# Second attention layer put into a software-pipelined order; GpSimd widens the reciprocals

## The chip, the cores and the metric

The kernel runs on one core of a Trainium2 chip. The metric is device time in microseconds (us). The core has five engines with a queue each: TensorE (PE), VectorE (DVE), ScalarE (ACT), GpSimd (POOL), and SyncE (SP), which issues the transfers. Each takes its instructions strictly in order and waits on semaphores for the others.

## The reference

16 entries of 128 rows by 512 go through two cross-attention layers. Layer 0 (16 heads, keys from the context and the entry itself) ends in a residual and a GELU MLP; its result is `y`. Layer 1, the one that the change touches, is a grouped attention with 32 query heads of 16 and 8 key heads:

```python
q = hidden_state @ Wq + bq
k = encoder_hidden_state @ Wk + bk
v = encoder_hidden_state @ Wv + bv
...
scores = jnp.einsum('bkgld,bksd->bkgls', q, k) * scale
scores = scores + encoder_attention_mask[:, :, None, :, :]
attn = jax.nn.softmax(scores, axis=-1)
out = jnp.einsum('bkgls,bksd->bkgld', attn, v)
...
out = out @ Wo + bo
x = out + hidden_state
mu = jnp.mean(x, axis=-1, keepdims=True)
var = jnp.var(x, axis=-1, keepdims=True)
return (x - mu) * jax.lax.rsqrt(var + EPS) * gamma + beta
```

## The kernel before

The program has three parts, one after the other with a barrier between: `attention` (layer 0), `mlp` and `second_attention` (layer 1). Products of fp32 are made of three passes over high and low halves (`split_product`, line 162). The weights of layer 1 are split into halves at its head (`take_hi` on ACT, `take_lo` on DVE).

`second_attention` works entry by entry. For entry e, in order of the data:

- `turn`: PE transposes the rows of `y` (line 1661), ACT writes `hThi` (1419), DVE `hTlo` (1505).
- `query`: PE makes 12 products (162), DVE adds the bias into `Qn` (1512). `turn_query`: PE transposes (1676), ACT and DVE write `QThi`, `QTlo`.
- `context`: PE makes 12 products for K and V, DVE writes `Cn` and `V` (1525, 1527). `turn_context`: PE transposes (1690), ACT writes `KThi` (1430), DVE `KTlo` (1534).
- `scores` in two rounds (1700), each filling four PSUM banks `S`. A round has four steps, so an entry has steps 0 to 7. In each step DVE adds the mask and takes the maximum (`mask_max`, 1548), ACT takes four exponentials with their sums (`exp`, 1441), PE transposes the probabilities (`probs`, 1710) into bank `O` or `T`, and DVE (1561, even steps) or ACT (1449, odd steps) copies them to `pT`.
- For each round: DVE takes the reciprocal of the sums (`invert`, 1555), PE transposes it (`inverse`, 1720), ACT copies it to `inv` (`spread`, 1455), PE multiplies with `V` (`values`, 1730), DVE scales (`attended`, 1568), POOL splits into `aThi` and `aTlo` (1376, 1378).
- `output`: 12 PE products in two halves (1743), DVE adds the residual (`res`, 1575), which POOL has prepared (`residual`, 1367). DVE takes the moments (1580 to 1591), POOL does three Newton steps (`root`, 1388), DVE normalises (`norm`, 1597), POOL applies gamma and beta (`affine`, 1395, 1397), SP stores.

Outside `S`, `O` and `T` two PSUM banks, `G` (the tiles J), are shared by all the rest. Each user waits for the semaphore of the former user's reader; in the kernel before, these waits are written out by hand.

What sets the order is a function `period(b)` on each engine, a hand-written list with operations of the entry before b, of b itself and of the one or two after it; `all_periods` runs it for b = -1 to 16, in a loop for the middle ones. The reciprocal is written 16 times wide by DVE itself, since the transposed copy is wanted on 16 rows for each head:

```python
nc.vector.reciprocal(rec[r][:, :, :], den[r][:, :].unsqueeze(2).broadcast_to([P, RC * EIGHT, DH1]))\
    .then_inc(rec_ready, 1)
```

Of the kernel before, what the change touches and what calls it, by code (L numbers as in the profile page):

```python
# [33 lines left out]
P = 128  # L34
# [10 lines left out]
SB = 4  # L45
# [1178 lines left out]

def all_periods(eng, period):

    for n in (-1, 0, 1):
        period(Entry(n))
    with eng.Fori(0, (B - 4) // 2) as it:
        period(Entry(2, it))  # L1230
        period(Entry(3, it))
    for n in (B - 2, B - 1, B):
        period(Entry(n))


def second_attention(nc, top, staging, ident, handed, banks, mask, q_b, k_b, v_b, o_b, norm_w, norm_b, out):
# [14 lines left out]
    with st:  # L1251
# [19 lines left out]
        rec = [sb(f"rec{r}", [P, RC * EIGHT, DH1]) for r in range(ROUNDS)]  # L1271
# [15 lines left out]
        a_seen, moments_seen, scores_seen = map(sem, ("a_seen", "moments_seen", "scores_seen"))  # L1287
# [6 lines left out]
        SMALL = 3  # L1294

# [8 lines left out]
        with nc.Block() as block:  # L1304

            @block.sync
            def _(sp):
                def load_context(e):
                    for h in range(2):
# [3 lines left out]
                def load_mask(e):  # L1313
                    sp.dma_start(madd[e.s][:, :], mask[e.index(), 0]).then_inc(mask_loaded[e.s], 16)

                def load_rows(e):
                    sp.dma_start(y_rows[e.s][:, :], kept_y[e.index()]).then_inc(y_loaded[e.s], 16)
# [4 lines left out]

                def period(b):
                    if b.exists() and b.plus(2).exists():
                        sp.wait_ge(resid_ready, b.count(1, 1))
                        sp.wait_ge(turned, b.count(1, 1))
                        load_rows(b.plus(2))
                        sp.wait_ge(c_full, b.count(1, 1))
                        load_context(b.plus(2))
                    if b.plus(-2).exists():  # L1330
                        store(b.plus(-2))
                    if b.exists() and b.plus(2).exists():
                        sp.wait_ge(masked, b.count(STEPS, STEPS))
                        load_mask(b.plus(2))
# [16 lines left out]
                store(Entry(B - 1))  # L1351
# [4 lines left out]
            def _(pool):  # L1356
# [22 lines left out]

                def root(e):  # L1380
# [18 lines left out]
                def period(b):  # L1399
                    if b.plus(-2).exists():  # L1400
                        root(b.plus(-2))
                    if b.plus(-1).exists():
                        attended(b.plus(-1), 1)
# [629 lines left out]
```

## Time and profile before

| | |
|---|---|
| median of 3 runs | 1276.95 us (1273.9 to 1278.49) |
| the profiled execution | 1279.8 us |
| its span | 1278.0 us |
| PE busy | 1121.2 us (88%) |
| DVE busy | 735.7 us (58%) |
| ACT busy | 658.9 us (52%) |
| POOL busy | 310.3 us (24%) |
| DMA, mean | 56 GB/s |

The shares are means over three different stages; the layer in question is the last third of the span. Busy time of PE counts matmuls that overlap by their starts, with modelled ends. Idle time in a wait is put down to the instruction that released it.

### The profile page before, as it was taken

How to read it: one execution, taken by the hardware profiler on the slowest of the kernel's cores; microseconds unless marked ns; L12 is line 12 of the kernel's file. 1: busy time of each engine (PE TensorE's matmuls, PEld its weight loads, DVE VectorE, ACT ScalarE, POOL GpSimd, SP SyncE). 2: the span in 40 equal slices, each digit the busy share in tenths (PEclk: the TensorE clock that was granted, in tenths of full speed). 3: DMA queues.
4: the chain of work that ended last, by engine and by line, in shares of the span. 5: the costliest groups of instructions: out<-in, count | busy, mean ns of one | idle time of the engine just before them, and what ended most of it. 6: DMA issues, size and time to landing. Idle time of an engine off the chain costs nothing. (4 is left out here: it accounts for less than half of the span.)

```text
span 1278.0 us, 27329 instructions
## 1 busy us (share of the span) xinstructions
PE 1121.2 (88%) x8976; PEld 935.1 (73%) x8976; DVE 735.7 (58%) x2667; ACT 658.9 (52%) x2220; POOL 310.3 (24%) x475
## 2 busy tenths in 40 slices
PE   4899999999999975999999999996778778778774
PEld 3788888888888854898989989985556556556553
DVE  4577777777776755422212212215678778788784
ACT  4455555555555544533333333325677677677672
POOL 1223333332332331000000000000133333333334
PEclk8999999999999987999999999997889989989987
DMA  6212111112111005211001101404111111111100
GB/s 242 86 55 69 45 43 43 43 47 81 44 43 43 26 17 174 90 50 50 30 20 49 50 0 49 116 17 116 32 59 36 53 52 35 56 49 35 45 10 25
DMA packets 65349, 71.10 MB, mean 56 GB/s; under 512 B 7056, under 2 KB 41104, under 8 KB 65296
## 3 DMA queue, kind: packets, MB, share of 16 engines
q1 hardware_dynamic: 65296, 70.42, 17.5%
q8 instruction: 30, 0.49, 0.2%
q14 instruction: 23, 0.19, 0.1%
HBM read 49.43 MB, written 20.97 MB: 55 GB/s over the span
## 5 line engine op out<-in xcount | busy, mean ns | idle before, releaser
L689 POOL TENSOR_TENSOR pr<-pr,rec 128x512 f32<-128x512 f32 x128 | 130.6, 1042 | 297.2 <-DVE rec L947 297.2
L1441 ACT ACTIVATE pr<-pr,nmax 128x128 f32<-128x128 f32 x512 | 198.1, 392 | 0.8
L1921 ACT ACTIVATE g_m<-J,b_part_m 128x256 f32<-128x256 f32 x128 | 60.6, 474 | 217.9 <-PE J L162 217.9
L791 ACT ACTIVATE pr<-pr,nmax 128x256 f32<-128x256 f32 x256 | 126.6, 501 | 4.1 <-DVE nmax L936 4.0
L1548 DVE CUSTOM_DVE_ANT_0 pr<-S,madd 128x128 f32<-128x128 f32 x512 | 115.7, 284 | 14.3 <-PE S L1700 10.3
L1898 POOL TENSOR_TENSOR resid_m<-resid_m,b_all_m 128x512 f32<-128x512 f32 x16 | 23.1, 1464 | 329.7 <-DMA resid_m<-in_x 329.7
L1441 ACT ACTIVATION_READ_ACCUMULATOR pr<-pr,nmax 128x1 f32 x512 | 98.4, 192 | 0.0
L936 DVE CUSTOM_DVE_ANT_0 pr<-S,madd 128x256 f32<-128x256 f32 x256 | 92.6, 418 | 8.2 <-PE S L1127 8.1
L162 PE MATMUL J<-wqhi,hThi 128*128 128x512 f32 x128 | 65.1, 508 | 22.6 <-DVE wqlo L150 11.3
L162 PE MATMUL J<-nT0hi_m,uphi_m 128*128 128x256 f32 x256 | 73.2, 286 | 9.8 <-DVE uplo_m L150 8.9
L162 PE MATMUL J<-hThi,wkhi 128*128 128x256 f32 x256 | 75.4, 294 | 5.9 <-DVE wvlo L150 5.9
L162 PE MATMUL J<-nT0hi_m,uplo_m 128*128 128x256 f32 x256 | 72.7, 284 | 0.0
L162 PE MATMUL J<-nT0lo_m,uphi_m 128*128 128x256 f32 x256 | 72.6, 283 | 0.0
L1710 PE MATMUL T<-ident,pr 128*128 128x128 f32 x256 | 42.0, 289 | 34.5 <-ACT pr L1441 34.5
L162 PE MATMUL J<-hThi,wklo 128*128 128x256 f32 x256 | 72.0, 281 | 0.0
L162 PE MATMUL J<-hTlo,wkhi 128*128 128x256 f32 x256 | 72.0, 281 | 0.0
L162 PE MATMUL J<-nT1hi_m,uphi_m 128*128 128x256 f32 x256 | 71.8, 280 | 0.0
L162 PE MATMUL J<-nT1hi_m,uplo_m 128*128 128x256 f32 x256 | 71.6, 280 | 0.0
L162 PE MATMUL J<-nT1lo_m,uphi_m 128*128 128x256 f32 x256 | 71.5, 279 | 0.0
L1145 PE MATMUL S<-ident,pr 128*128 128x128 f32 x512 | 62.9, 277 | 0.0
L162 PE MATMUL J<-wqlo,hThi 128*128 128x512 f32 x128 | 61.8, 483 | 0.0
L1455 ACT ACTIVATE inv<-J 128x256 f32<-128x256 f32 x32 | 12.3, 384 | 94.2 <-PE J L1720 94.2
(232 smaller groups left out, 3323.1 us busy)
## 6 DMA issues: line engine op xcount, KB each, us to landing
staged<-in_L_xattn_mlp_w SPq DMA_DIRECT2D x16, 512.0 KB, 5.1
rows<-in_ctx SPq DMA_DIRECT2D x16, 256.0 KB, 2.8
rows<-in_x SPq DMA_DIRECT2D x16, 256.0 KB, 3.0
kept_c<-hThi SPq DMA_DIRECT2D x16, 256.0 KB, 2.6
kept_c<-hTlo SPq DMA_DIRECT2D x16, 256.0 KB, 2.8
kept_n<-n_out SPq DMA_DIRECT2D x16, 256.0 KB, 2.4
n_in<-kept_n SPq DMA_DIRECT2D x16, 256.0 KB, 3.7
resid_m<-in_x SPq DMA_DIRECT2D x16, 256.0 KB, 2.9
```

What stands on the lines that cost most here:

```text
L162: mm = nc.tensor.matmul(out, stationary(a, k), moving(b, k), start=first and k == 0 and (a, b) == PASSES[0], stop=last and k == chunks - 1 ...
L689: pool.tensor_tensor(part, part, by.unsqueeze(2).broadcast_to([P, per_bank, keys]), ALU.mult).then_inc(normed, 1)
L791: last = nc.scalar.activation(part, part, ACT.Exp, bias=nmax[slot][:, at], scale=-1.0, accum_out=den[slot][:, at])
L936: last = nc.vector.tensor_tensor_reduce(pr[slot][:, j, cols], S[j][:, cols], madd[s][:, :], -1.0, FAR, ALU.add, ALU.min, nmax[slot][:, j * ...
L1145: mm = nc.tensor.transpose(S[j][:, to * P:(to + 1) * P], pr[slot][:, j, q * P:(q + 1) * P], ident[:, :])
L1441: last = nc.scalar.activation(pr[k][:, i, :], pr[k][:, i, :], ACT.Exp, bias=nmax[k][:, i:i + 1], scale=-1.0, accum_out=den[r][:, at:at + 1])
L1455: nc.scalar.activation(inv[r][:, :], G[r][:, 0:RC * R], ACT.Copy).then_inc(r_spread, 1)
L1548: last = nc.vector.tensor_tensor_reduce(pr[k][:, i, :], S[j][:, i * R:(i + 1) * R], madd[e.s][:, :], -1.0, FAR, ALU.add, ALU.min, nmax[k][ ...
L1710: mm = nc.tensor.transpose(PT[t][:, i * R:(i + 1) * R], pr[k][:, i, :], ident[:, :])
L1898: pool.tensor_tensor(resid[t][:, :], resid[t][:, :], b2_all[:, :], ALU.add)\
L1921: nc.scalar.activation(g[slot][:, :], J[j][:, 0:PR], ACT.Gelu_apprx_tanh, bias=b1_part[:, f, :]).then_inc(J_taken[j], 1)
```

## The change

1. Each operation of the layer gets a place in the period and an entry, from two ahead (`turn`, `query`, `turn_query`, `context`) over one ahead (`turn_context`, the first steps) to one behind (`output`, `moments`, `root`) and two behind (`norm`, `affine`, `store`). `all_periods` now runs from -2 to 17, and nothing is left outside it.
2. A table (`HOME`) gives each operation one of the two banks: `values` of round 0 moves from the bank of `inverse` 0 to the other, `turn_context` too, `context` and `output` change to bank 0. PE's waits for a free bank are derived from the table and the order (`free`). `values` 0 no longer waits for `inv`.
3. `invert` gives 16 values per partition, and POOL copies them 16 wide (`widen`), for PE's `inverse`.
4. The bank of a copy of step k is written as `k % 2`; which engine copies is as before.
5. SP's loads of mask, rows and context are placed by entry, with waits of their own.

```diff
+def at(b, ahead, operation, *which):
+
+    e = b.plus(ahead)
+    if e.exists():
+        operation(e, *which)
...
-    for n in (-1, 0, 1):
+    for n in range(-2, 4):
         period(Entry(n))
...
-        rec = [sb(f"rec{r}", [P, RC * EIGHT, DH1]) for r in range(ROUNDS)]
+        rec = [sb(f"rec{r}", [P, RC * EIGHT]) for r in range(ROUNDS)]
+        wide = [sb(f"wide{r}", [P, RC * EIGHT, DH1]) for r in range(ROUNDS)]
...
+        HOME = dict(turn=1, query=0, turn_query=0, context=0, turn_context=1, inverse0=0, inverse1=1, values0=1,
+                    values1=1, output=0)
+        ORDER = (("turn", 2), ("output", -1), ("turn_context", 1), ("inverse0", 0), ("values0", 0), ("query", 2),
+                 ("inverse1", 0), ("turn_query", 2), ("values1", 0), ("context", 2))
...
                 def period(b):
...
+                    if not first_two(b.plus(1)):
+                        at(b, 1, load_mask)
+                    if not first_two(b.plus(2)):
+                        at(b, 2, load_rows)
+                    if not first_two(b.plus(2)):
+                        at(b, 2, load_context)
+                    at(b, -2, store)
...
+                def widen(e, r):
+                    pool.wait_ge(rec_ready, e.count(ROUNDS, r + 1))
+                    wait(pool, r_full, e.count(ROUNDS, r - 1))
+                    pool.nop().then_inc(rec_seen, 1)
+                    pool.tensor_copy(wide[r][:, :, :], rec[r][:, :].unsqueeze(2).broadcast_to([P, RC * EIGHT, DH1]))\
+                        .then_inc(rec_wide, 1)
...
+                    at(b, -1, attended, 1)
+                    at(b, 1, residual)
+                    at(b, 0, widen, 1)
+                    at(b, -2, affine)
+                    at(b, 0, attended, 0)
+                    at(b, -1, root)
+                    at(b, 1, widen, 0)
...
-                    nc.vector.reciprocal(rec[r][:, :, :], den[r][:, :].unsqueeze(2).broadcast_to([P, RC * EIGHT, DH1]))\
-                        .then_inc(rec_ready, 1)
+                    wait(dve, rec_wide, e.count(ROUNDS, r - 1))
+                    nc.vector.reciprocal(rec[r][:, :], den[r][:, :]).then_inc(rec_ready, 1)
...
-                turn(Entry(0))
                 for u in QUERY + (CONTEXT,):
                     staging.take_lo(nc, dve, u, targets[u])
                 dve.wait_ge(consts_loaded, 96)
                 dve.wait_ge(prepared, 3)
                 all_periods(dve, period)
-                norm(Entry(B - 1))
...
                 def values(e, r):
-                    pe.wait_ge(r_spread, e.count(ROUNDS, r + 1))
+                    free(f"values{r}", e)
...
+                    at(b, 2, turn)
+                    at(b, 0, probs, 3)
+                    at(b, -1, output, 0)
+                    at(b, 1, turn_context)
+                    at(b, 0, probs, 4)
+                    at(b, -1, output, 1)
+                    at(b, 0, probs, 5)
+                    at(b, 1, scores, 0)
+                    at(b, 0, probs, 6)
+                    at(b, 0, inverse, 0)
+                    at(b, 0, values, 0)
+                    at(b, 0, probs, 7)
+                    at(b, 2, query)
+                    at(b, 1, probs, 0)
+                    at(b, 0, inverse, 1)
+                    at(b, 1, scores, 1)
+                    at(b, 2, turn_query)
+                    at(b, 1, probs, 1)
+                    at(b, 0, values, 1)
+                    at(b, 1, probs, 2)
+                    at(b, 2, context)
```

Three places show what stands in the queues. On ACT, in the last period before the loop, around `inv` of round 0; before:

```order
L1441 ACTIVATE pr_1,den_1<-pr_1,nmax_1 128x128 x3
L1449 ACTIVATE pT_1<-T 128x512 [waits o_full_1,p_full1_1]
L1441 ACTIVATE pr_1,den_1<-pr_1,nmax_1 128x128 [waits masked_1]
L1441 ACTIVATE pr_1,den_1<-pr_1,nmax_1 128x128 x3
L1430 ACTIVATE KT0hi<-J,parity 128x128 [waits ct_full_1]
L1430 ACTIVATE KT0hi<-J,parity 128x128
L1455 ACTIVATE inv_1<-J 128x256 [waits a_scaled_1,r_full_1]
L1441 ACTIVATE pr_1,den_1<-pr_1,nmax_1 128x128 [waits masked_1]
L1441 ACTIVATE pr_1,den_1<-pr_1,nmax_1 128x128 x3
L1449 ACTIVATE pT_1<-T 128x512 [waits o_full_1,p_full1_1]
```

and now (L1466 is the exponential, L1474 the copy of probabilities, L1480 `inv`):

```order
L1466 ACTIVATE pr_1,den_1<-pr_1,nmax_1 128x128 [waits masked_1]
L1466 ACTIVATE pr_1,den_1<-pr_1,nmax_1 128x128 x3
L1474 ACTIVATE pT_1<-T 128x512 [waits o_full_1,p_full1_1]
L1466 ACTIVATE pr_1,den_1<-pr_1,nmax_1 128x128 [waits masked_1]
L1466 ACTIVATE pr_1,den_1<-pr_1,nmax_1 128x128 x3
L1480 ACTIVATE inv_1<-J 128x256 [waits a_scaled_1,r_full_1]
L1466 ACTIVATE pr_1,den_1<-pr_1,nmax_1 128x128 [waits rec_ready_1,masked_1]
L1466 ACTIVATE pr_1,den_1<-pr_1,nmax_1 128x128 x3
L1466 ACTIVATE pr_1,den_1<-pr_1,nmax_1 128x128 [waits masked_1]
L1466 ACTIVATE pr_1,den_1<-pr_1,nmax_1 128x128 x3
L1474 ACTIVATE pT_1<-T 128x512 [waits o_full_1,p_full1_1]
L1466 ACTIVATE pr_1,den_1<-pr_1,nmax_1 128x128 [waits masked_1]
```

Before, `inv` stood ahead of the exponentials of step 6, and `KThi` ahead of `inv`; now the exponentials of step 7 are ahead of it, and behind it come those of the next entry, steps 0 and 1.

On PE, the same place of the program, behind the scores of the next entry's first round; before (T is a bank for odd steps, O for even ones):

```order
L1700 MATMUL S<-KT0lo,QT0hi 128x256 x4
L1700 MATMUL S<-KT0hi,QT0lo 128x256 x4
L1720 MATMUL J<-ident,rec_1 128x128 [waits rec_ready_1,a_scaled_1]
L1720 MATMUL J<-ident,rec_1 128x128
L1710 MATMUL T<-ident,pr_1 128x128 [waits copied1_1,exped_1]
L1710 MATMUL T<-ident,pr_1 128x128 x3
L1730 MATMUL J<-pT_1,V_1 32x256 [waits copied1_1,copied0_1,r_spread_1]
L1730 MATMUL J<-pT_1,V_1 32x256 x7
L1710 MATMUL O<-ident,pr_1 128x128 [waits copied0_1,exped_1]
L1710 MATMUL O<-ident,pr_1 128x128 x3
L1661 MATMUL J<-ident,y_rows 128x128 [waits res_ready_1,y_loaded1]
```

and now:

```order
L1707 MATMUL S<-KT0lo,QT0hi 128x256 x4
L1707 MATMUL S<-KT0hi,QT0lo 128x256 x4
L1717 MATMUL O<-ident,pr_1 128x128 [waits copied0_1,exped_1]
L1717 MATMUL O<-ident,pr_1 128x128 x3
L1724 MATMUL J<-ident,wide_1 128x128 [waits rec_wide_1,res_ready_1]
L1724 MATMUL J<-ident,wide_1 128x128
L1734 MATMUL J<-pT_1,V_1 32x256 [waits copied1_1,copied0_1,k_ready_1]
L1734 MATMUL J<-pT_1,V_1 32x256 x7
L1717 MATMUL T<-ident,pr_1 128x128 [waits copied1_1,exped_1]
L1717 MATMUL T<-ident,pr_1 128x128 x3
L162 MATMUL J<-wqhi,hThi 128x512 [waits r_spread_1,h_ready_1]
```

`values` had to wait for `r_spread`, ACT's copy of the transposed reciprocals; now for `k_ready`, the former reader of its bank. `turn` is gone from the end of the period, and the query products of the entry two ahead stand behind the transposes of step 7.

On DVE, at the head of the layer; before:

```order
L1501 TENSOR_REDUCE parity<-ident 128x1 x2
L1505 TENSOR_TENSOR hTlo<-J,hThi 128x512 [waits h_hi_1]
L150 TENSOR_TENSOR wqlo<-staged,wqhi 128x1024 [waits staged_hi] x2
L150 TENSOR_TENSOR wclo<-staged,wchi 128x1024 [waits staged_hi]
L1512 TENSOR_TENSOR Qn<-J,bq_all 128x8x4x16 [waits q_full_1,prepared_1,consts_loaded_1]
L1517 SCALAR_TENSOR_TENSOR QT0lo<-J,QT0hi 128x512 [waits q_hi_1]
```

and now:

```order
L1513 TENSOR_REDUCE parity<-ident 128x1 x2
L150 TENSOR_TENSOR wqlo<-staged,wqhi 128x1024 [waits staged_hi] x2
L150 TENSOR_TENSOR wclo<-staged,wchi 128x1024 [waits staged_hi]
L1517 TENSOR_TENSOR hTlo<-J,hThi 128x512 [waits h_hi_1,prepared_1,consts_loaded_1]
L1524 TENSOR_TENSOR Qn<-J,bq_all 128x8x4x16 [waits q_full_1]
L1529 SCALAR_TENSOR_TENSOR QT0lo<-J,QT0hi 128x512 [waits q_hi_1]
```

`hTlo` of entry 0 stood first; now it is behind the three splits of weights, and the wait for all constants has moved from `Qn` to it.

## Rows read from the trace of the kernel before

**Rows 1.** Stages. Columns: window, us, busy us (x instructions) per engine, TensorE clock, DMA share, GB/s
```profile
860.10:898.22 38.12, 21.55 (x135) 16.90 (x136) 23.36 (x93) 19.84 (x64) 3.10 (x5) 0.76 0.38 111
898.22:1233.17 334.95, 265.25 (x2254) 199.71 (x2254) 260.42 (x1225) 233.49 (x1036) 111.68 (x251) 0.92 0.14 44
1233.17:1278.00 44.83, 26.21 (x188) 16.60 (x188) 23.81 (x100) 19.98 (x90) 20.43 (x51) 0.71 0.05 19
```

**Rows 2.** Waits in 898.22 to 1233.17: engine, line, waited for: total us, times, longest
```profile
ACT inv L1455 <- PE J L1720: 88.4, 28, 3.9
...
DVE hTlo L1505 <- ACT hThi L1419: 43.9, 14, 4.4
...
PE T L1710 <- ACT pr L1441: 31.5, 14, 2.3
```

**Rows 3.** Groups by line, second layer: busy us, mean ns | idle before
```profile
L1441 ACT ACTIVATE pr<-pr,nmax 128x128 f32<-128x128 f32 x512 | 198.1, 392 | 0.8
...
L1555 DVE RECIPROCAL rec<-den 128x256 f32<-128x256 f32 x32 | 55.9, 1746 | 0.0
...
L1376 POOL CAST aT1hi<-an 128x256 fp32r<-128x256 f32 x16 | 6.5, 407 | 77.3 <-DVE an L1568 72.9 <-issue 4.3
...
L1585 DVE TENSOR_SCALAR stat<-stat 128x1 f32<-128x1 f32 x16 | 2.5, 154 | 0.6
```

**Rows 4.** Timeline of ACT, one period: start, us, instruction, idle before and releaser
```profile
1115.23 0.38 ACT L1455 ACTIVATE inv<-J 128x256 f32<-128x256 f32 x1 [3.49 <-PE J L1720]
```

**Rows 5.** Timeline of PE, same period
```profile
1108.95 0.47 PE L1743 MATMUL J<-wohi,aT0hi 128*128 128x512 f32 x1 [0.37 <-issue]
...
1111.89 0.39 PE L1743 MATMUL J<-wolo,aT0hi 128*128 128x512 f32 x1
1112.12 0.40 PE L1743 MATMUL J<-wohi,aT0lo 128*128 128x512 f32 x1
1113.84 0.39 PE L1700 MATMUL S<-KT0hi,QT0hi 32*128 32x256 f32 x4 [1.33 <-DVE KT0lo L1534]
...
1115.66 1.07 PE L1730 MATMUL J<-pT,V 128*32 128x256 f32 x16
...
1120.66 0.65 PE L1710 MATMUL T<-ident,pr 128*128 128x128 f32 x4 [2.30 <-ACT pr L1441]
```

**Rows 6.** That period in seven windows, columns as in the stages
```profile
1098.69:1102.10 3.41, 3.41 (x9) 2.65 (x9) 3.41 (x15) 1.65 (x8) 2.61 (x12) 0.50 0.00 0
...
1115.75:1119.17 3.42, 2.07 (x24) 1.19 (x24) 0.37 (x5) 2.65 (x11) 0.00 (x0) 1.00 0.55 186
1119.17:1122.58 3.41, 1.51 (x8) 1.14 (x9) 3.15 (x17) 3.41 (x18) 0.67 (x2) 1.00 0.13 44
sum 23.89, PE 18.91 PEld 14.22 DVE 18.79 ACT 16.73 POOL 8.48; mean PE 2.70 PEld 2.03 DVE 2.68 ACT 2.39 POOL 1.21
```

**Rows 7.** Tile y_rows in 898 to 1233: landing of its loads
```profile
DMA to landing us min/median/max: 2.6/2.7/2.7
```

**Rows 8.** Timeline of DVE, head of the second layer
```profile
863.06 0.69 DVE L1505 TENSOR_TENSOR hTlo<-J,hThi 128x512 fp32r<-128x512 f32 x1 [0.95 <-ACT hThi L1419]
...
872.43 0.69 DVE L1512 TENSOR_TENSOR Qn<-J,bq_all 128x512 f32<-128x512 f32 x1 [4.93 <-DMA nb_all<-in_L_xattn_beta]
```

**Rows 9.** Timeline of PE, same stretch
```profile
866.42 0.79 PE L162 MATMUL J<-wqhi,hThi 128*128 128x512 f32 x1 [4.03 <-DVE wqlo L150]
...
870.69 0.40 PE L162 MATMUL J<-wqhi,hTlo 128*128 128x512 f32 x1
...
879.02 0.39 PE L1700 MATMUL S<-KT0hi,QT0hi 32*128 32x256 f32 x4 [1.36 <-DVE KT0lo L1534]
```

**Rows 10.** Timeline of POOL, last entries
```profile
1262.85 1.29 POOL L1395 TENSOR_TENSOR fin<-nrm,nw_all 128x512 f32<-128x512 f32 x1
...
1269.03 0.46 POOL L1388 TENSOR_TENSOR stat<-stat 128x1 f32<-128x1 f32 x2 [3.54 <-DVE stat L1591]
...
1272.01 0.20 POOL L1388 TENSOR_TENSOR stat<-stat 128x1 f32<-128x1 f32 x1
```

More of the change, by code:

```diff
@@ L1294, in second_attention, with bank @@
         SMALL = 3
+        HOME = dict(turn=1, query=0, turn_query=0, context=0, turn_context=1, inverse0=0, inverse1=1, values0=1,
+                    values1=1, output=0)
+        ORDER = (("turn", 2), ("output", -1), ("turn_context", 1), ("inverse0", 0), ("values0", 0), ("query", 2),
+                 ("inverse1", 0), ("turn_query", 2), ("values1", 0), ("context", 2))
+        EMPTIED = dict(turn=(h_ready, 1, 1), query=(q_added, 1, 1), turn_query=(q_ready, 1, 1), context=(c_ready, 1, 1),
+                       turn_context=(k_ready, 1, 1), inverse0=(r_spread, 2, 1), inverse1=(r_spread, 2, 2),
+                       values0=(a_scaled, 2, 1), values1=(a_scaled, 2, 2), output=(res_ready, 1, 1))
+        def bank(use):
+            return G[HOME[use]]
         u0, end = staging.first[2], staging.first[3]
@@ L1652, in _, with free @@
                 all_periods(dve, period)
-                norm(Entry(B - 1))
             @block.tensor
             def _(pe):
+                def free(use, e):
+                    at_ = [name for name, _ in ORDER].index(use)
+                    b = e.plus(-ORDER[at_][1])
+                    for back in range(1, 3 * len(ORDER)):
+                        periods, n = divmod(at_ - back, len(ORDER))
+                        name, ahead = ORDER[n]
+                        user = b.plus(periods + ahead)
+                        if HOME[name] == HOME[use] and user.exists():
+                            sem_, per, more = EMPTIED[name]
+                            pe.wait_ge(sem_, user.count(per, more))
+                            return
                 def turn(e):
                     pe.wait_ge(y_loaded[e.s], e.uses(16))
-                    wait(pe, res_ready, e.count(1, -2))
+                    free("turn", e)
                     for k in range(KC):
-                        mm = nc.tensor.transpose(G[1][:, k * R:(k + 1) * R], y_rows[e.s][:, k * P:(k + 1) * P],
+                        mm = nc.tensor.transpose(bank("turn")[:, k * R:(k + 1) * R], y_rows[e.s][:, k * P:(k + 1) * P],
                                                  ident[:, :])
@@ L1688, in turn_context @@
                     pe.wait_ge(c_ready, e.count(1, 1))
-                    pe.wait_ge(q_ready, e.count(1, 1))
-                    nc.tensor.transpose(G[0][:, 0:R], Cn[:, :], ident[:, :]).then_inc(ct_full, 1)
+                    free("turn_context", e)
+                    nc.tensor.transpose(bank("turn_context")[:, 0:R], Cn[:, :], ident[:, :]).then_inc(ct_full, 1)
                 def scores(e, r):
@@ L1775, in period @@
-                    if b.exists():
-                        probs(b, 4)
-                    if before.exists():
-                        output(before, 1)
-                    if after.exists():
-                        scores(after, 0)
-                    if b.exists():
-                        inverse(b, 0)
-                        probs(b, 5)
-                        values(b, 0)
-                        probs(b, 6)
-                    if b.plus(2).exists():
-                        turn(b.plus(2))
```

245 lines of the change are left out of this document (85 added, 160 removed).

## The prediction

> **What bounds the kernel now.** I read the stages first. The second layer's steady part, from the scores of entry 1 to those of entry 15, takes 334.95 us for 14 periods, 23.9 each, and the 860 us before the layer are two stages that the change leaves alone [rows 1]. In that part no engine is full: divided by 14, PE is busy 18.9 us a period, DVE 18.6, ACT 16.7, POOL 8.0. So the layer is not held by one engine's work but by the order in which three nearly equal engines wait for one another, and the waits say where [rows 2]: ACT stands 88.4 us in 28 waits of `inv` (6.3 a period) for PE's transpose of the reciprocals, DVE 43.9 us (3.1 a period) in `hTlo` for ACT, PE 31.5 us (2.2 a period) in the transposes of the last probabilities for ACT's exponentials. These are one circle. The reciprocal takes DVE 1.75 us [rows 3]; until it is done PE can't transpose it and ACT, which has `inv` next in its queue, does nothing [rows 4]; all exponentials behind it are late, so PE idles before step 7's transposes [rows 5], and `turn` is late for DVE.
>
> One thing comes on top: after the stretch in which PE does little but transposes and waits (1.51 us busy of 3.41), its clock drops from 2.4 to 1.2 GHz for 3.41 us, and the next period's query products run there [rows 6]. The other six windows of that period are at 1.00. PE was full in the slow one, so 1.7 of its 3.41 us are the price.
>
> **The change, part by part.**
> 1. *Reciprocal of 16 values, not 256.* Removes 2 x 1.746 us of DVE a period [rows 3]. The trace has no reciprocal of 16; its ends are a tiny DVE operation (0.154 us) and the old one (1.746). A sixteenth of the elements is nearest to the tiny one; I take 0.2. DVE's work: 18.6 - 3.5 + 0.4 = 15.5 us.
> 2. *GpSimd widens.* Two copies to 128x256 a period. Nearest row is the cast of 128x256, 0.41 us [rows 3]; POOL becomes 8.0 + 0.8 = 8.8 us, a third of its time. What stands behind them: `widen` 1 waits for the reciprocal with `affine` and `attended` 0 behind it, `widen` 0 stands behind the Newton steps (some 3.2 us). Both have several us before PE wants them, since the PE order puts `inverse` half a period later.
> 3. *The reciprocals' transpose no longer stands before ACT's next exponentials.* `inv` of round 1 moves behind steps 0 to 2 of the next entry, `inv` of round 0 behind step 7. The 6.3 us of ACT's waits go. ACT's work is unchanged: 16.7 us a period.
> 4. *`turn` and `query` two ahead, in one period; `values` of round 0 in the other bank.* PE's matmuls are the same. Its busy time of 18.9 us minus the 1.7 of the slow window is 17.2 us at full clock; matmul records overlap a little, so 17.2 is an upper end and 16.7 about a lower one.
> 5. *SP's loads.* Each is now issued behind `store` of an entry that waits for `affine`. By POOL's order `affine` ends some 12 us into a period and the rows are wanted by `turn` at the start of the next; landing takes 2.7 us at most [rows 7]. Hidden, with about 1 us to spare.
>
> The floor of the period is then 16.7 (ACT) to 17.2 (PE). I walked one new period, with these durations (an exponential step is 4 x 0.392 = 1.57 us [rows 3]; on PE four transposes 0.5, `values` 1.0, products of 512 columns 0.23 each from start to start [rows 5]), and met five places where PE can wait: `turn_context` for `hTlo` behind step 4's exponentials, `output` for `context` at the seam, `scores` of the next entry for `KTlo` (before: 1.33 us), transposes 7 for `exp` 7 (before: 2.30 us [rows 5]), `context` for `QTlo`. Each has another operation as cover and leaves 0 to 0.4 us. Counted from PE's `turn`, in us: output half 0 at 1.1, `turn_context` 2.6, transposes 4 at 2.7, output half 1 at 3.2, transposes 5 at 4.7, `scores` of the next entry at 5.4, transposes 6 at 6.3, `inverse` 0 and `values` 0 at 6.8 and 7.1, transposes 7 at 8.1, `query` from 8.6 to 11.4, then transposes 0, `inverse` 1 and `scores` 1 until 13.1, `turn_query`, transposes 1, `values` 1 and transposes 2 until 15.5, `context` until 17.0. ACT is through at 16.3 and DVE, which ends with `context`, at 17.6, that is 0.6 into the next. The walk closes at 17.0; it knows no sequencer time for the waits, of which PE showed 0.37 us before one output [rows 5]. With 0.5 us for such, I take **17.5 us a period**. The gain is 14 x (23.9 - 17.5) = 90 us.
>
> *Head.* All `turn` are now inside the periods, and DVE enters them after a wait for all six constants. So the first `hTlo`, at 863.1 before, runs when the constants are there, which was 872.4 [rows 8]. The query products (866.4 to 871.1 [rows 9]) start at about 873.1 and end at 877.8; before, their reader could start at 872.4. That is 5.4 us lost. `context` 0 then waits for the query's bank use (`q_ready`), 1.7 more, and entry 1's `turn` stands ahead of `turn_context` 0, 0.7 more. I take +7.5 us; the ends are +5.4, and +10 if entry 1's products, which were beside nothing else, hold the next scores up too.
>
> *Tail.* From scores of entry 15 to the end 44.8 us [rows 1]. `widen`, `affine` 13 and Newton 14 (2.6 and 3.2 us [rows 10]) now stand ahead of POOL's last split; against that, ACT's two waits of `inv` (6.3 us) fall away. I take -1.5, ends -6 and +5.
>
> Sum: 1278.0 - 90 + 7.5 - 1.5 = 1194.0 us span; with the 1.8 us around the span 1195.8 for this execution (1279.8). The median shown, 1276.95, is 0.22% below it: **1193 us**.
>
> **A rule that speaks against it.** What the rows show: the clock fell after a stretch with transposes, waits and four products [rows 6], and stayed up after one with 16 `values` products and eight transposes. The new period has as many transposes, but in the PE order never more than two such groups stand between products. So the sum has full clock. The Trainium skill (TensorE: Matmul & The Clock Gate, on transposes) says that transposes don't count as PE work for the clock. By that rule, the trace agreeing so far, a denser queue of transposes and idle moments need not keep the clock up; the next rival is what it would make.
>
> **The rivals.**
> - *A slow window in each period stays.* It costs 1.7 us of a PE that is now nearly full, so the period is 17.5 + 1.7 = 19.2 at most, 18.7 if the other waits hide in it; I take 18.9. For: the new stretch from step 5 to step 7 has only `scores` and `values` as products. Against: the window with `values` as its only products was followed by one at 1.00 [rows 6]. Time: 1193 + 14 x 1.4 = 1213.
> - *The interlocks are tighter than my walk.* Three engines at 88% or more of a period of 17.5, each strictly in order: any late one is everybody's. If the waits add 3 to 4 us to the floor in place of 0.5, the period is 20 to 21 and the time 1228 to 1242. For: the waits shown are all on another engine [rows 2], and three such engines were kept 5 us apart from their work before. Against: the places above have cover.
> - *Slower than before: GpSimd as the bound.* The widened copy reads each value 16 times, a form that the trace doesn't have. PE's `inverse` 1, the whole queue behind it and SP's loads behind `affine` hang on it. It decides once POOL's sum passes 23.8 us: (23.8 - 8.0) / 2 = 7.9 us a copy, 19 times the cast. At 8.2 us the period is 24.4, the time 1277 + 14 x 0.5 + 6 = 1290. Against: its longest operation in the layer takes 1.29 us, for two inputs of twice the size [rows 10].
> - *No difference.* It needs a period of 23.5 us, so that removed waits return elsewhere (the 1.7 us of the clock and 4 us of interlocks). Nothing in the rows points there.
>
> **How the numbers follow.** Forecast (period 16.9 to 18.1) 0.55, slow window 0.25, tight interlocks 0.15, no difference 0.02, slower 0.03. A measurement can tell 0.3%, 4 us. The low end is the floor period, 14 x 0.7 = 10 us below: 1183. The high end takes in the slow window with the dearer head: 1220. Faster 0.95, same 0.02, slower 0.03.
>
> **What would show it.** Right: in the profile after, scores of successive entries 17 to 18 us apart; a RECIPROCAL group near 0.2 us; ACT's wait for `inv` under 1 us a period; PE clock 1.0 in the steady part; first scores at about 887; POOL copies near 0.4 us. Wrong: a regular 0.50 window, PE waits for `hTlo`, `KTlo` or `y_rows` over 1 us a period, or POOL over 12 us a period.

## The result, and the profile after

The changed kernel takes **1179.33 us** (median of 4 runs, 1176.5 to 1182.09) against 1277.65 for the kernel before beside it: ratio 0.9236, 95% interval 0.9205 to 0.9266. The forecast was 1193, with a range from 1183 to 1220. The direction was right, and the time came out below the low end.

Stages of the profiled execution after (1182.09 us, span 1179.4), cut at the same events as [rows 1]: the entry-1 scores, the entry-15 scores, the end. Columns as there.

```profile
857.85:905.11 47.26, 24.25 (x142) 19.44 (x142) 23.13 (x94) 21.11 (x70) 3.49 (x6) 0.68 0.31 89
905.11:1139.48 234.37, 232.97 (x2252) 182.68 (x2252) 216.02 (x1224) 229.51 (x1038) 118.62 (x277) 0.99 0.19 62
1139.48:1179.40 39.92, 20.62 (x185) 13.38 (x184) 20.30 (x101) 18.59 (x86) 23.86 (x56) 0.86 0.07 27
```

The middle row is the result: 14 periods in 234.37 us, 16.74 each, where there were 334.95 us, 23.93 each. (The first of them takes 18.09 us; TensorE's granted clock in it is 0.52 until 909. The other 13 take 16.64 each.) PE is busy 232.97 of 234.37 us (99.4%), ACT 97.9%, DVE 92.2%. PE's sum came down from 265.25 to 232.97 us with the same instructions. About half of that is the clock: old_clock below has 267.02 us at full clock, of which its 84 extra products are about 19 (an estimate, 0.23 us each), so some 248 are left. The rest fits how records are counted, though no run isolates it: a product with a break behind it counts 0.39 us, one that is followed at once 0.23.

From PE's first `turn` of the layer (861.76 before, 859.51 after) the head to entry 1's scores took 36.5 us before and takes 45.6, +9.1. The tail went from 44.8 to 39.9, -4.9. Together: 1278.0 - 100.6 + 9.1 - 4.9 = 1181.6; the remaining 2.3 us lie ahead of the layer, in code that is the same in both.

What [rows 2] showed is gone. The waits of PE, and the longest ones of ACT and DVE, in the steady part after (engine, line, waited for: total us, times, longest); first PE:

```profile
PE J L1666 <- DMA y_rows<-kept_y: 0.6, 2, 0.4
PE J L1746 <- DVE V L1539: 0.2, 1, 0.2
```

then ACT:

```profile
ACT QT0hi L1449 <- PE J L1682: 2.4, 5, 1.1
ACT QT1hi L1449 <- PE J L1682: 1.0, 5, 0.2
ACT hThi L1444 <- PE J L1666: 0.5, 2, 0.3
ACT inv L1480 <- PE J L1724: 0.3, 1, 0.3
```

then DVE:

```profile
DVE Qn L1524 <- PE J L162: 7.5, 14, 1.2
DVE pr L1560 <- issue: 2.3, 6, 1.3
```

ACT's 88.4 us for `inv` are 0.3, DVE's 43.9 for `hTlo` 0.2, PE's 31.5 for the last exponentials none. The groups that answer to the reciprocal and the cast of [rows 3], steady part:

```profile
L1407 POOL COPY wide<-rec 128x256 f32<-128x256 f32 x28 | 11.1, 397 | 41.3 <-DVE rec L1568 39.0 <-POOL stat L1418 2.3
...
L1568 DVE RECIPROCAL rec<-den 128x16 f32<-128x16 f32 x28 | 6.9, 245 | 0.0
```

And one period in windows, as [rows 6]; the clock is 1.00 in all five, and PE is busy throughout in four of them:

```profile
1006.54:1009.95 3.41, 3.41 (x52) 2.51 (x52) 3.18 (x18) 3.41 (x17) 1.28 (x1) 1.00 0.00 0
1009.95:1013.36 3.41, 3.41 (x22) 2.65 (x21) 2.98 (x23) 3.41 (x18) 2.71 (x3) 1.00 0.00 0
1013.36:1016.77 3.41, 3.41 (x54) 2.53 (x54) 3.13 (x14) 3.28 (x16) 2.50 (x10) 1.00 0.47 130
1016.77:1020.18 3.41, 3.41 (x27) 3.21 (x26) 3.34 (x19) 3.41 (x14) 2.58 (x9) 1.00 0.54 196
1020.18:1023.59 3.41, 3.35 (x33) 2.55 (x34) 3.41 (x22) 3.41 (x19) 0.00 (x0) 1.00 0.00 0
```

### The profile page after: what moved, and what is told of

It is laid out like the page before. It is cut to its first block and busy times, and to the rows that moved or that the text cites. A ratio compares the mean times of both kernels' runs of the same rounds, so it can differ in the third digit from the quotient of the medians.

```text
span 1179.4 us, 27363 instructions
## 1 busy us (share of the span) xinstructions
PE 1086.9 (92%) x8976; PEld 918.5 (78%) x8976; DVE 688.2 (58%) x2667; ACT 654.9 (56%) x2220; POOL 321.0 (27%) x507
## 3 DMA queue, kind: packets, MB, share of 16 engines
q1 hardware_dynamic: 65296, 70.42, 18.9%
## 5 line engine op out<-in xcount | busy, mean ns | idle before, releaser
L1466 ACT ACTIVATE pr<-pr,nmax 128x128 f32<-128x128 f32 x512 | 199.1, 402 | 3.2 <-DVE nmax L1560 3.2
L1466 ACT ACTIVATION_READ_ACCUMULATOR pr<-pr,nmax 128x1 f32 x512 | 103.3, 202 | 0.0
L162 PE MATMUL J<-wqhi,hThi 128*128 128x512 f32 x128 | 56.0, 438 | 18.3 <-DVE hTlo L1517 10.9
L1145 PEld LDWEIGHTS S<-ident,pr 128*128 128x128 f32 x512 | 59.0, 144 | 2.2 <-issue 0.2
L162 PEld LDWEIGHTS J<-nT0hi_m,uphi_m 128*128 128x128 f32 x256 | 49.0, 192 | 12.9 <-issue 9.3
L162 PEld LDWEIGHTS J<-hThi,wkhi 128*128 128x128 f32 x256 | 48.6, 190 | 7.7 <-DVE wvlo L150 5.0
```

The lines of the kernel that those rows point to most:

```text
L162: mm = nc.tensor.matmul(out, stationary(a, k), moving(b, k), start=first and k == 0 and (a, b) == PASSES[0], stop=last and k == chunks - 1 ...
L1145: mm = nc.tensor.transpose(S[j][:, to * P:(to + 1) * P], pr[slot][:, j, q * P:(q + 1) * P], ident[:, :])
L1466: last = nc.scalar.activation(pr[k][:, i, :], pr[k][:, i, :], ACT.Exp, bias=nmax[k][:, i:i + 1], scale=-1.0, accum_out=den[r][:, at:at + 1])
```

## The experiments

**How they are read.** The second layer began anywhere from 856 to 867 us in these executions, in code that no edit touches. So the period is read from the trace of each (start of entry 1's scores to start of entry 15's, over 14), and the medians stand beside it where there were rounds; a time without a ratio is a single execution. How far a period repeats can be seen in new_head and new_head_tail, whose steady part is that of the changed kernel: 16.75 and 16.77 beside 16.74. Two theories stood against each other. *Order*: the old time went through waits in a circle, and the new period is PE's own work, with nothing on top. *Part*: the narrow reciprocal, or the clock, brought most of it.

### The parts of the change, alone

**old_narrow**: the order of before with the narrow reciprocal.

```diff
+                def widen(e, r):
...
+                    pool.tensor_copy(wide[r][:, :, :], rec[r][:, :].unsqueeze(2).broadcast_to([P, RC * EIGHT, DH1]))\
...
-                    nc.vector.reciprocal(rec[r][:, :, :], den[r][:, :].unsqueeze(2).broadcast_to([P, RC * EIGHT, DH1]))\
-                        .then_inc(rec_ready, 1)
+                    nc.vector.reciprocal(rec[r][:, :], den[r][:, :]).then_inc(rec_ready, 1)
```

GpSimd does `widen` of round 1 first in its period, and of round 0 ahead of `attended(b, 0)`.

> The order of before, with one part of the change alone: DVE takes the reciprocal of 16 values and GpSimd widens it. Theory (the time went through the circle of waits, PE's transpose of the reciprocals standing before ACT's next exponentials): the circle gets shorter by what leaves DVE in it, 1.75 - 0.25 - 0.40 = 1.1 us at each of two rounds, less what the two more hand-overs cost. The period falls from 23.9 us by 1 to 2.5 us, so 14 x 1 to 2.5 = 14 to 35 us less than before, about 1255; ACT still waits 4 to 5 us a period for its copy inv. Rival (the narrow reciprocal is what brought the gain, the order little): most of the 98 us, a time under 1215.

Measured: 1267.6 us, ratio 0.991 (0.9877 to 0.9943); period 23.20, 0.73 us less. The theory's lower end was missed, and the rival's gain of most of 98 us is far off. Why so little? ACT's wait in old_narrow, 899.59 to 1224.37:

```profile
ACT inv L1468 <- PE J L1733: 79.2, 28, 3.6
```

It hardly fell from 88.4. PE's timeline of the kernel before shows what the releaser's name hid:

```profile
1121.72 0.50 PE L162 MATMUL J<-wqhi,hThi 128*128 128x512 f32 x1 [0.41 <-DVE an L1568]
...
1125.88 0.45 PE L162 MATMUL J<-wqhi,hTlo 128*128 128x512 f32 x1
1126.17 0.60 PE L1710 MATMUL O<-ident,pr 128*128 128x128 f32 x4
1126.61 0.38 PE L1720 MATMUL J<-ident,rec 128*128 128x128 f32 x2
```

and DVE's, the reciprocal beside them:

```profile
1123.95 1.74 DVE L1555 RECIPROCAL rec<-den 128x256 f32<-128x256 f32 x1
```

The reciprocal ended at 1125.7, under twelve query products that stood ahead of its transpose in PE's queue until 1126.2. In this round (round 1) the 1.75 us of the reciprocal were nearly free: the wait was PE's order.

In round 0 too the transpose waited for something else. The reciprocal on DVE and the transpose on PE, in the kernel before:

```profile
1110.06 1.75 DVE L1555 RECIPROCAL rec<-den 128x256 f32<-128x256 f32 x1
...
1113.10 0.61 DVE L1534 SCALAR_TENSOR_TENSOR KT0lo<-J,parity,KT0hi 128x128 fp32r<-128x128 f32 x2
...
1114.75 0.44 PE L1720 MATMUL J<-ident,rec 128*128 128x128 f32 x2
```

It was done at 1111.8, and PE transposed it 2.9 us later, behind the scores that waited for `KT0lo` [rows 5]. `KT0lo` stands behind the reciprocal in DVE's queue, so the wide reciprocal did cost something here, but through DVE's own queue. In old_narrow DVE gets only a part of the 1.5 us back, because the copy behind the reciprocal then waits 0.85 us for PE; what is left is about the 0.73 us of the period:

```profile
1106.37 0.69 DVE L1574 COPY pT<-O 128x512 f32<-128x512 f32 x1 [0.85 <-PE O L1723]
```

**new_wide**: the new order with the wide reciprocal back on DVE (the reverse of the diff above).

> The new order with that one part undone: DVE writes the reciprocals wide again (1.75 us each), GpSimd widens nothing. Theory (the new period is at the floor of the busiest engine): DVE's 15.4 us a period become 15.4 + 2 x 1.5 = 18.4 us, more than PE's 16.6, so DVE sets the period at 18.4 to 18.9 us: 14 to 15 periods x 1.8 = 25 to 32 us slower than the changed kernel, about 1207. Rival (the order gives all of it and has room for the wide reciprocals): within 5 us of 1179. Second rival (the order closes only with the narrow reciprocal): a period over 20 us, over 1225.

Measured: 1213.72 us, ratio 0.9491 (0.9437 to 0.9545), period 18.73.

```profile
905.21:1167.43 262.22, 237.81 (x2251) 182.79 (x2250) 253.89 (x1224) 233.34 (x1038) 108.37 (x249) 1.00 0.17 55
```

The columns are as in the stages: PE, PEld, DVE, ACT, POOL. DVE, the third, is now 253.89 of 262.22 us, 97%, and sets the pace. The period is inside the expected 18.4 to 18.9; the time is 34 us above the changed kernel's, not 25 to 32, and 4.4 of them lie in the tail (44.27 against 39.92 us). Of the 7.19 us that the change takes from a period, the order alone gives 5.20 and the reciprocal alone 0.73; the other 1.26 are there only with both. The reciprocal is worth 1.99 us in the new order, because there DVE would be the fullest engine.

**old_clock**: the kernel before, with filler on PE before step 7's transposes; its result is overwritten.

```diff
+                def filler(e):
+                    pe.wait_ge(copied[1], e.count(SB, 3))
+                    for _ in range(6):
+                        nc.tensor.matmul(PT[1][:, :], wq[0][:, 0, 0:P], wq[0][:, 0, :], start=True, stop=True)
```

> The kernel before, with six products of 512 columns more a period (their result is never used, and is overwritten), which PE does while it would wait for the last exponentials. Theory A (the half-speed window of every period cost about 1.7 us beside the waits, and came after a stretch in which PE did little but transposes): the granted clock stays at 1.00 in the second layer and the period falls from 23.9 to about 22.2 us, 24 us less. Rival B (the window fell into the time that the circle of waits had to spare, or more work does not keep the clock up): the period stays at 23.9 us or grows by up to 1.4 us (the six products), 0 to +20 us.

Measured: 1268.18 us, ratio 0.9922 (0.9894 to 0.995), period 23.35, granted clock 0.99 in the steady part (0.92 before). More work on PE made the kernel faster. So the clock theory holds in kind, but the window cost 0.57 us a period here, not 1.7. The filler itself is not in that number: it fits into PE's wait before step 7's transposes, of which 12.2 us in 14 are left. What takes the place of the slow products is the wide reciprocal, for which PE's transpose now waits 5.8 us in 13 periods:

```profile
1097.05 0.44 PE L1725 MATMUL J<-ident,rec 128*128 128x128 f32 x2 [0.38 <-DVE rec L1555]
```

**old_narrow_clock**: both.

> The order of before with both edits at once, the narrow reciprocal widened by GpSimd and the six unused products a period on PE. Alone they gave 0.73 and 0.57 us a period. Theory (each hid the other: at ACT's wait for round 0 the wide reciprocal ended at 1125.7 and PE's query products, at half speed, at 1126.2, so that removing one leaves the other): together they give clearly more than the sum of 1.3, 2.0 to 3.0 us a period, 28 to 42 us, about 1243. Rival (they are independent): 1.3 us a period, about 1259. Second rival (the order itself is the limit, both are small change): under 1 us a period, over 1263.

Measured: 1247.2 us, ratio 0.976 (0.9712 to 0.9808), period 21.91: 2.02 us less, where 0.73 + 0.57 = 1.30 was the sum. The two hid each other, at the theory's lower end. The trace is of the fastest of the six executions (1238.5 us), so the medians matter here: against the kernel before they give 30.4 us for both, 10.8 and 10.2 for each alone, the same picture.

**old_spread_later**: the kernel before, ACT's `inv` one place later.

```diff
                         copy(before, 7)
                     if b.exists():
                         exp(b, 1)
+                        exp(b, 2)
                     if before.exists():
                         spread(before, 1)
                     if b.exists():
-                        exp(b, 2)
                         copy(b, 1)
                         exp(b, 3)
                     if after.exists():
...
                         for u in OUT:
                             staging.take_hi(nc, act, u, targets[u])
                     if b.exists():
-                        spread(b, 0)
                         exp(b, 6)
+                        spread(b, 0)
                         copy(b, 5)
                     if b.plus(2).exists():
                         turn(b.plus(2))
```

> The kernel before with ACT's copy inv one place later in both rounds: behind the next entry's third exponential step in place of before its third (round 1), and behind the copy of step 5 (round 0). Nothing else moves. Theory (the reciprocals' place in ACT's queue alone makes the circle): ACT has work while it would wait, its wait of 6.3 us a period falls by 1 to 3, and the period by 0.5 to 2 us, 7 to 28 us less. Rival (the wait is only moved: values of the same bank and DVE's attended wait for inv instead, and PE's transposes are as late as before): within 5 us of before.

(That text puts round 0's copy behind the copy of step 5; it is ahead of it, behind the exponentials of step 6, as the diff shows.)

Measured: 1267.27 us, ratio 0.9925 (0.9897 to 0.9953), period 23.01, 0.91 less. ACT's wait in 899 to 1230 halved,

```profile
ACT inv L1455 <- PE J L1720: 44.4, 27, 2.5
```

but of the 44 us that it lost only 13 came off the time. Removing part of a wait's total didn't bring that much off the time.

**old_three**: all three in the old order.

> The order of before with the narrow reciprocal, the six unused products a period, and ACT's copy inv one place later in both rounds. The first two together gave 2.0 us a period, the last alone 0.9. Theory (waits that hide one another: each edit gives more once the others are made): 3.3 to 4.5 us a period, a period of 19.5 to 20.6, about 1222. Rival (they add up): 2.9 us, a period of 21.0, about 1236. Second rival (they overlap, the remainder is held by another circle of the old order): under 2.5 us, a period over 21.4.

Measured: 1231.52 us, ratio 0.9638 (0.9602 to 0.9675), period 21.12: 2.81 us less, against 2.02 + 0.91 if they add up. So the theory of the text above (3.3 to 4.5) fails and its first rival holds: this pair adds up. (The medians, 48.8 us against 30.4 + 10.3, don't contradict it within their intervals.) The other 4.4 us down to 16.74 belong to the rest of the order: in old_three, 899 to 1180, these waits stand:

```profile
DVE hTlo L1518 <- ACT hThi L1432: 35.5, 14, 3.8
...
ACT hThi L1432 <- PE J L1674: 22.1, 14, 2.2
ACT inv L1468 <- PE J L1738: 21.2, 13, 1.7
DVE pT L1574 <- PE O L1723: 17.2, 26, 1.5
```

The first two are `turn`. Both orders do it for the entry two ahead, but on PE the old one has it behind step 6's transposes and the new one before those of step 3, three steps earlier. Whether its move alone takes these waits away was not tried.

### What bounds the new period

**new_pe_more**: four unused products more before step 0's transposes, `nc.tensor.matmul(PT[t][:, :], wq[0][:, 0, 0:P], wq[0][:, 0, :], start=True, stop=True)` each.

> The changed kernel with four products of 512 columns more a period on PE (their result is never used), 4 x 0.23 = 0.93 us by the rows. Theory (PE bounds the period, with no slack): the period grows by 0.93 to about 17.6 us, the time by about 14 us, and PE stays at 98 to 99% busy. Rival (the period closes through waits between the engines, and PE has cover): the period grows by under 0.4 us.

Measured: 1193.4 us, period 17.61, +0.87. PE busy 245.40 of 246.57 us. The theory holds.

**new_pe_less**: four products fewer.

```diff
-                    split_product(nc, bank("query")[:, :], lambda h, k: hT[h][:, k, :], lambda h, k: wq[h][:, k, :], KC)
+                    for k in range(KC):
+                        for h in range(2):
+                            mm = nc.tensor.matmul(bank("query")[:, :], hT[0][:, k, :], wq[h][:, k, :],
+                                                  start=k == 0 and h == 0, stop=k == KC - 1 and h == 1)
```

> The changed kernel with one of three passes of the query product left out (the pass of the low half of the hidden rows; the output is a little less exact): 4 products, 0.93 us of PE a period. Theory (PE bounds now, ACT at 16.4 us a period is right behind it): the period falls only to ACT's sum, 16.4 to 16.6 us, the time by 2 to 5 us, and PE shows waits for ACT. Rival (ACT has more room than its busy time says): the period falls by the full 0.93 us to 15.8, 13 us less.

Measured: 1182.42 us, period 16.38, -0.36 (its layer began at 866.95, 7.4 us later than in the changed kernel, which hides the gain in its time).

```profile
910.05:1139.37 229.32, 221.00 (x2195) 172.07 (x2195) 216.62 (x1224) 228.18 (x1038) 118.47 (x277) 0.99 0.19 63
```

ACT, the fourth column, 228.18 of 229.32 us, takes over. Between PE's bound and ACT's lie 0.36 us.

**new_act_more**: two copies of a bank more on ACT, `nc.scalar.activation(spare[k // 2][:, :], PT[k % 2][:, :], ACT.Copy)` in steps 1 and 3.

> The changed kernel with two copies of a transpose bank to an unused tile more a period on ACT, about 0.5 us each. Theory (ACT has 0.3 us a period to spare under PE's 16.7): the period becomes ACT's new sum, 16.4 + 1.0 = 17.4 us, so about +0.7 us a period, +10 us, and PE waits for exponentials. Rival (PE alone sets the period, and ACT's waits have more cover): within 4 us of 1179.

Measured: 1191.66 us, period 17.41, +0.67; ACT busy 242.24 of 243.76 us. ACT can be filled to 99.4% as PE can.

**new_dve_more**: two copies more on DVE, ahead of the real copies of steps 0 and 2.

```diff
+                    if k in (0, 2):
+                        nc.vector.tensor_copy(spare[k // 2][:, :], PT[k % 2][:, :])
                     nc.vector.tensor_copy(pT[r][:, j, :, :, :].rearrange("p c a k -> p (c a k)"), PT[k % 2][:, :])
```

> The changed kernel with two copies of a transpose bank to an unused tile more a period on DVE, about 0.6 us each. Theory (DVE has 1.3 us a period to spare): its sum becomes 15.4 + 1.2 = 16.6 us, just PE's; the time grows by 0 to 6 us. Rival (each late DVE operation is everybody's): the whole 1.2 us a period, +17 us.

Measured: 1196.08 us, period 17.58, +0.84. A miss: DVE's busy time left 1.3 us a period, its sum rose by only 1.0 (230.07 against 216.02 us), and the period by 0.84. Two runs ask why.

**new_dve_free**: two additions behind the real copies, from data in SBUF, so that no bank is held.

```diff
                         .then_inc(copied[k % 2], 1)
+                    if k in (0, 2):
+                        nc.vector.tensor_tensor(spare[k // 2][:, :], wq[0][:, 0, :].bitcast(F32), wq[0][:, 1, :].bitcast(F32), ALU.add)
```

> The changed kernel with two additions of 128x512 to an unused tile more a period on DVE, at the same places as the two copies that cost 0.84 us a period, but behind the real copy of the bank and from other data, so that no bank is held longer. Theory A (the copies cost by holding PE's transpose banks for 0.6 us more): now under 0.3 us a period, about 1183. Rival B (DVE's queue has only 0.5 us of waiting in it, the rest of its idle time is gaps between dependent small operations that no work can fill): again 0.6 to 0.9 us a period, 9 to 13 us in all.

Measured: 1195.45 us, period 17.56, +0.82. The held bank is out.

**new_dve_seam**: one such addition, in `query` before `dve.wait_ge(q_full, e.count(1, 1))`.

> The changed kernel with one such addition a period, just before DVE's query, where it waits 0.54 us for PE. By either theory that wait takes it up: the period grows by 0 to 0.2 us, under 3 us in all. Against (DVE has no room at any place): 0.6 us, 9 us in all.

Measured: 1180.27 us, period 16.85, +0.11. DVE's wait for the query (7.5 us in the changed kernel) is 0.6 here:

```profile
DVE Qn L1526 <- PE J L162: 0.6, 1, 0.6
```

So DVE has room at one place, the 0.54 us in front of `Qn`, and next to none elsewhere. In new_dve_free that wait is still there:

```profile
DVE Qn L1525 <- PE J L162: 7.3, 14, 1.0
```

Work put behind that wait doesn't use it. What it does instead shows on PE, in new_dve_more:

```profile
PE J L1749 <- DVE V L1540: 5.1, 13, 0.8
```

(5.0 us in new_dve_free, 0.2 in the changed kernel.) `V` is the end of DVE's period, and PE's `output` needs its bank. So the added work makes `V` late, PE and its next query late with it, and the wait in front of `Qn` is as long as before. This reading fits the three runs; no run moves `V` alone.

**new_samebank**: `values0=0` in the table of banks for `values0=1`.

> The changed kernel with its other table entry put back: the values of round 0 go to the bank of the inverse of round 0, as before, and not to the other one. Theory (PE is full and each of its waits is paid in full): values 0 follows inverse 0 in the same bank and must wait until ACT has copied the inverse, some 0.7 to 1.2 us, and a transpose stands behind it; the period grows from 16.7 by 0.7 to 1.5 us, 10 to 22 us slower than the changed kernel, 1190 to 1200. Rival (there are 0.3 us of slack on ACT and 1.3 on DVE, PE catches up elsewhere): within 4 us of 1179.

Measured: 1200.04 us, ratio 0.9386 (0.9337 to 0.9435), period 18.09, +1.35. PE's timeline of one period:

```profile
1052.14 1.07 PE L1734 MATMUL J<-pT,V 128*32 128x256 f32 x16 [0.89 <-ACT inv L1480]
...
1054.01 0.47 PE L162 MATMUL J<-wqhi,hThi 128*128 128x512 f32 x1 [0.21 <-DVE an L1581]
```

PE waits 0.89 + 0.21 us at the two places foreseen; the whole costs 20.7 us. Putting back that one number in the table costs a fifth of the change's gain.

### Head and tail, and a kernel that beats both

**new_head**: only the three constants loaded first are awaited by DVE, at its first `query`.

```diff
+        early = sem("early")
...
+                    first = frm is q_b or frm is k_b or frm is v_b
-                    sp.dma_start(to, frm.partition_broadcast(P)).then_inc(consts_loaded, 16)
+                    sp.dma_start(to, frm.partition_broadcast(P)).then_inc(early if first else consts_loaded, 16)
...
+                    if e.it is None and e.n == 0:
+                        dve.wait_ge(early, 48)
```

> The changed kernel, with its head mended: DVE waits before its first operations of the layer for no constants, and at its first query for the three constants that are loaded first, not for all six. Theory (the head's loss is DVE's wait of 6.2 us for the last constant): the first hTlo comes about 6 us earlier and with it the first scores, 6 us less: ratio to the changed kernel 0.995, about 1173.5. Rival (PE or ACT is late next in the head: takes of the weights, context behind the query): under 3 us.

Measured: 1173.74 us over 6 runs, ratio 0.9176 (0.9138 to 0.9214). From the layer's first `turn` to entry 1's scores: 39.5 us, 6.1 less than in the changed kernel, as expected. DVE's timeline in the changed kernel showed the wait:

```profile
870.24 0.69 DVE L1517 TENSOR_TENSOR hTlo<-J,hThi 128x512 fp32r<-128x512 f32 x1 [6.17 <-DMA nb_all<-in_L_xattn_beta]
```

Three of the head's 9.1 us remain. They go with the new place of `query` and `turn` there; no run takes them apart.

**new_head_tail**: the same head, and this order in the last two periods.

```diff
+                        at(b, -1, attended, 1)
+                        at(b, 0, widen, 1)
+                        at(b, 0, attended, 0)
+                        at(b, -2, affine)
+                        at(b, 0, attended, 1)
+                        at(b, -1, root)
```

> The same head, and at the end another order on GpSimd: in the last two periods the splits of entry 15's rows go before the affine of entry 13 and the Newton steps of entry 14. Theory (PE's last two output halves each wait 1.8 us for the split, behind 2.6 and 3.2 us of such work): both waits go, and the end comes 3 to 5 us earlier than in the one before: about 1169.5. Rival (affine and Newton of the entries before are now late, and hold DVE's norm and the last output): 0 to +3 us.

Measured: 1172.41 us over 6 runs, ratio 0.9171 (0.9133 to 0.921). Its tail takes 38.65 us, 1.3 less than new_head's 39.93, not 3 to 5; the medians (1.3 us apart, intervals almost the same) can't tell the two kernels apart, so this gain is the trace's alone. PE's waits for the splits (1.76 and 1.81 us) became one of 1.42, but in DVE's timeline the norm of entry 14, which stands ahead of the last output, now waits longer for GpSimd's Newton steps (4.32 in the changed kernel):

```profile
1162.17 0.55 DVE L1624 TENSOR_SCALAR nrm<-res,stat 128x512 f32<-128x512 f32 x1 [5.69 <-POOLq L1422]
```

Theory and rival were both half right. By the medians this kernel is 7 us faster than the changed one and 105 us faster than before. Against the changed kernel the two intervals of the ratio still touch (0.9205 and 0.921), so the 7 us rest on the traces as well: 6.0 us in the head (39.57 against 45.60) and 1.3 in the tail.

## Why the prediction was right or wrong

**What bounds the kernel.** Right: an order of waits, and no engine's work. The part of it laid on the reciprocal ("until it is done PE can't transpose it") was wrong for both rounds. It was done 0.9 us before its transpose in round 1, which stood behind the query products, and 2.9 us before it in round 0, which stood behind the scores; the narrow reciprocal alone gave 0.73 us a period.

**Part 1**, reciprocal 0.2 us: 0.245. DVE's work 15.5 us a period: 15.4. **Part 2**, widening 0.41: 0.397; POOL 8.8 a period: 8.5. **Part 3**, ACT's 6.3 us of waits go: they went (0.3 us in all). **Part 5**, loads of SP hidden: 0.6 us of PE's waits in 14 periods.

**Part 4 and the period: the step that failed.** The forecast set 17.5 us: the walk's 17.0 and 0.5 "for sequencer time". Measured 16.74, of which PE's work is 16.64. The 0.5 is not there: PE's waits are 0.8 us in all 14 periods. What it does show as "issue" stands on weight loads,

```profile
PEld O L1717 <- issue: 6.0, 15, 0.4
```

and loads overlap the products before them. The walk itself, which closes at 17.0, is also too long, in the stretch from `turn` to the next scores. PE in one period of the changed kernel:

```profile
1056.46 0.39 PE L1707 MATMUL S<-KT0hi,QT0hi 32*128 32x256 f32 x4
...
1068.03 0.60 PE L1666 MATMUL J<-ident,y_rows 128*128 128x128 f32 x4
1068.47 0.60 PE L1717 MATMUL T<-ident,pr 128*128 128x128 f32 x4
1068.91 0.50 PE L1746 MATMUL J<-wohi,aT1hi 128*128 128x512 f32 x1
...
1073.21 0.39 PE L1707 MATMUL S<-KT1hi,QT1hi 32*128 32x256 f32 x4
```

From the scores to `turn` it takes 11.57 us, where the walk has 11.6; from `turn` to the scores 5.18 (4.81 in the period from 1001.75), where the walk has 5.4. Four transposes in that stretch last 0.44 us from start to start, not 0.5. So of PE's two ends, 16.7 and 17.2, the lower was the true one. The difference is 10.6 us, 14 times 0.76.

**The range.** Its low end, 1183, took the period alone, and 0.7 us under the forecast, where the floor named beside it (16.7) is 0.8 under. The period's miss by itself, 10.6 us, leads from 1193 to 1182.4, already outside. The head cost 9.1 against 7.5 (6.1 for the constants, forecast 5.4), the tail gave 4.9 against 1.5, and the time ahead of the layer lay 2.3 us lower in this execution: head and tail within their own bounds, and none of the three in the low end. The misses of head and tail have opposite signs, so they partly hide each other in the time. The sum of the forecast, put right: 1194.0 - 10.6 + 1.6 - 3.4 - 2.3 = 1179.3, the span.

**The rivals.** *Slow window stays*: no; 1.00 in the whole steady part from 909 on (0.52 in the 3.9 us before). Six products in the place of a wait restored it even in the old order (old_clock), and the new order has it with as many transposes as before and no filler. The rule of the Trainium skill (TensorE: Matmul & The Clock Gate, on transposes), that they don't count as PE work for the clock, is neither borne out nor against the rows: no run took the transposes apart from the waits. The price of the slow window was sized wrong for the old order, though: 0.57 us a period alone, not 1.7. *Tighter interlocks*: no, but near: one bank number gives back 1.35 us a period. *GpSimd as bound*: no, 0.397 us a copy against the 7.9 from which it would decide. *No difference*: no.

## What to carry to other kernels

When no engine is full, sum each engine's work at full clock and take the largest sum as the aim; an order in which every wait has other work in front of it reached it here within 1% (16.74 against 16.64), so an allowance on top of a closed walk needs a row that shows it on the engine that bounds. The releaser that a profile names is the last link only: look at what stands ahead of it in the same queue before crediting a shorter operation with a whole wait, since two delays that end within 0.5 us of each other are each worth little alone (0.73 and 0.57) and more together (2.02). Once an order is that tight, spare time is a place and not a sum: 0.68 us of DVE work cost 0.11 us in front of a wait and about 0.4 elsewhere.

## What the hardware showed beyond that

The two DVE experiments with additions from SBUF slowed GpSimd, which has the same instructions in all three. One of GpSimd's groups in the changed kernel, steady part (busy us, mean ns):

```profile
L1427 POOL TENSOR_TENSOR fin<-fin,nb_all 128x512 f32<-128x512 f32 x12 | 15.4, 1282 | 0.9
```

and in new_dve_seam:

```profile
L1428 POOL TENSOR_TENSOR fin<-fin,nb_all 128x512 f32<-128x512 f32 x12 | 21.4, 1785 | 0.9
```

Each of the 12 takes 0.50 us longer, beside a DVE addition of 0.69 us. In new_dve_free GpSimd's sum rises from 118.6 to 132.5 us; with the copies from PSUM in new_dve_more it stays at 119.2. In new_dve_free it is the Newton steps that meet the additions; one of their forms goes from 190 to 365 ns. The Trainium skill (SBUF — State Buffer, Who interferes with whom) says that a DVE instruction with two SBUF inputs contends with a GpSimd instruction that reads SBUF, through a lock on a shared pair of ports. The trace agrees: in one period DVE's addition runs from 1010.09 to 1010.78 and GpSimd's, which starts at 1010.14, takes 1.78 us instead of 1.28. DVE's time alone doesn't do it, since the copies from PSUM last as long (0.68 us); whether the number of the inputs or their place decides, the runs don't say. Nothing was lost by it in the period: new_dve_more costs as much without it (0.84 against 0.82 us).

Also not expected: a kernel became faster by 0.8% through more work (old_clock), six products whose results nobody reads, 1.4 us of PE a period, done where it would have waited.
